# Scales of a tile moved ahead of its row transfers on GpSimd, and the weights of its sums applied by two small instructions, in a GroupNorm and patch top-k kernel

## The chip, the cores and the metric

One core of a Trainium2 chip. The metric is the device time of one launch in microseconds (us). Times of single instructions, and spans, come from one profiled execution.

## What is computed

x has shape (4, 256, 256, 256), float32: four images, 256 channels, 256 x 256 pixels.

```python
def _gn(v, G=32, eps=1e-5):
    g = v.reshape(B_, G, C_ // G, H_, W_)
    m, s = mean and variance of g over axes (2, 3, 4)
    return ((g - m) / sqrt(s + eps)).reshape(v.shape)

def _L0_conv_ref(x):               # P = 32, k = C // 2 = 128
    s = 0.5 * _grad_mag(x) + 0.5 * abs(x)
    sp = s.reshape(n, C, 8, 32, 8, 32).mean(axis=(3, 5)).reshape(n, C, 64)
    ranks = argsort(argsort(-sp, axis=1), axis=1)
    mask = ranks < k
    return x * mask, each mask value over its 32 x 32 patch

out = x + _L0_conv_ref(_gn(x))
```

`_grad_mag` is |x(h, w+1) - x(h, w-1)| + |x(h+1, w) - x(h-1, w)| with zeros outside the image. So for each of 64 patches of an image the 128 channels with the largest score get their normalized values added, and the others stay x.

## The kernel before

**Tiles.** A tile is 16 channels of one image, 8 bands of 32 rows each, so 128 partitions (channel and band) with 8 patches of 1024 pixels in a partition: 4096 KB. There are 16 tiles to an image and 64 in all. Four tile buffers (`ring`) are in turn loaded, worked on and stored by the sync queue. During the first eleven tiles it also sends copies of the last image's first tiles from input to output.

**The work of a tile.** VectorE takes the statistics (`bn_stats`), the inner horizontal differences (`inner_across`, L669), and reductions of what others prepare. TensorE forms vertical differences of five patches, ScalarE sums absolute values, GpSimd forms the vertical differences of the other three patches (`difference`, L320), the columns next to patch borders (`end_columns`, L328) and the edges. The 8 kinds of sums of a tile lie in `sums[tile % RING]`. `total` (L699, L703) multiplies them by a table of weights (1, except 2 for LARGER and -512 for MEANS) and adds them over the kinds. `score` multiplies by the tile's scale and puts out a score for each patch and channel.

**The scale.** VectorE's `minus_mean` (L660) opens a tile. GpSimd's `partition_spread` (L372, L374, L376, with a `drain` after the first two) makes the term of the variance, TensorE's `variance` averages it over the group, VectorE's `stable_variance` (L694) adds eps, and GpSimd's `scales` (L383 to L394, with five drains) raises to the power -1/2, refines that by one Newton step and stores the scale and the factors. TensorE's `variance` stands ahead of all its vertical differences of the tile, and `stable_variance` ahead of most of VectorE's work of the tile. VectorE waits for `scale_ready` of the tile before it overwrites `var` or makes the tile's score.

**The choice.** From the ninth tile of an image on, the 16 largest scores left of each patch are taken after each tile (`pick`, `choices`). The rows chosen go into `rows`, four columns of 128 row numbers to a block, 16 blocks to an image, 64 in all. For a block GpSimd gathers four times 128 rows of 4 KB from the input by indirect DMA (`gather_block`, L350), ScalarE scales them (`finish_place`, L570), and GpSimd scatters them to the output (`scatter_block`, L365). One block is gathered in each tile from the eleventh on, and one is scattered from the thirteenth on; the last ten blocks follow behind the last tile. The last four tiles of an image are dense: the kernel keeps them in the ring, ScalarE scales those that the choice names (`finish_dense`, L580) and they are stored in halves; rows of them are left out of the gathers. ScalarE's order of a tile begins with `o0`, the finish of the block that was gathered in the tile before, and its order holds three `p` steps, which need GpSimd's differences, and six `v` steps, which need TensorE's.

**Order on the queues.** Each engine works in the order written. On GpSimd it is the loop at L396. The sync queue, in each tile: store of this tile, perhaps a copy, the halves of the dense tile before, and the load of the tile three ahead; this load waits until the tile before is summed by ScalarE, is stored, and its differences and edges are read. Gathers and scatters go through the software queue, loads and stores through the hardware queue.

Of the kernel before, what the change touches and what calls it, by code (L numbers as in the profile page):

```python
# [8 lines left out]
ALU = mybir.AluOpType  # L9
# [10 lines left out]
PARTS = 128  # L20
# [52 lines left out]
ROWS = IMAGES * TILES * PARTS * COLS  # L73
LARGER, ENDS, MEANS, ACROSS_LAST, DOWN, CENTRED, ROWS_AT_EDGE, COLUMNS_AT_EDGE = range(8)
KINDS = 8
WEIGHTS = {LARGER: 2.0, MEANS: -2.0 * (BN // 2)}

ORDER = "o0 a0 o1 v0 o2 a1 o3 p0 a2 v1 a3 a4 v2 a5 p1 a6 v3 a7 v4 p2 v5".split()
ORDER_DENSE = ("o0 a0 o1 v0 o2 a1 o3 p0 a2 v1 a3 d0 d1 v2 d2 d3 a4 p1 d4 a5 v3 d5 d6 a6 d7 v4 a7 p2 v5"
# [36 lines left out]
def groupnorm_patch_topk(nc: bass.Bass, x: bass.AP, out: bass.AP):  # L116

    ctx = ExitStack()
    with ctx:
        def sb(name, shape, dt=FP32):  # L120
            return ctx.enter_context(nc.sbuf_tensor(name, shape, dt))
# [24 lines left out]
        same_band = sb("same_band", [PARTS, BANDS])  # L146
        same_band16 = sb("same_band16", [PARTS, BANDS], BF16)
        minus_half = sb("minus_half", [PARTS, 1])
        weights = sb("weights", [PARTS, KINDS])
        place_numbers = sb("place_numbers", [PATCHES, 1], INT32)  # L150
        first_row = sb("first_row", [PATCHES, 1])
        group_numbers = sb("group_numbers", [PARTS, 2, TILES], INT32)
# [2 lines left out]
        record = [sb(f"record{b}", [PARTS, 3]) for b in range(RING)]  # L155
        all_sums = sb("sums", [PARTS, RING, KINDS, COLS])
        sums = [all_sums[:, b] for b in range(RING)]
        weighed = sb("weighed", [PARTS, KINDS, COLS])
        totals = sb("totals", [PARTS, COLS])
        spread = sb("spread", [PARTS, 1])  # L160
        away = sb("away", [PARTS, 1])
# [69 lines left out]

        block = ctx.enter_context(nc.Block())

        CONSTANTS = 26 + len(WEIGHTS)

        x_rows = x.rearrange("t p (w f) -> (t p w) f", w=COLS)
        out_rows = out.rearrange("t p (w f) -> (t p w) f", w=COLS)
# [29 lines left out]
        def _(pool):  # L267
            steps = [0]

            def make(ins):  # L270
                steps[0] += 1
                ins.then_inc(constants, 1)
                pool.wait_ge(constants, steps[0])
# [8 lines left out]
            make(nc.gpsimd.memset(minus_half[:], -0.5))  # L282
            make(nc.gpsimd.memset(all_sums[:], 0.0))
            make(nc.gpsimd.memset(factors[:], 0.0))
            make(nc.gpsimd.memset(weights[:], 1.0))
            for kind, weight in WEIGHTS.items():
                make(nc.gpsimd.memset(weights[:, kind:kind + 1], weight))
            make(nc.gpsimd.memset(same_channel[:], 1.0))
            make(nc.gpsimd.memset(averager[:], 0.0))
            make(nc.gpsimd.memset(plus[:], 0.0))  # L290
# [23 lines left out]
            def difference(tile, k):  # L314

                m = POOL_DOWN * tile + k
                if m >= PLACES:
                    pool.wait_ge(place_free, m - PLACES + 1)
                v = patch(ring[tile % RING], PE_DOWN + k)
                nc.gpsimd.tensor_tensor(place[m % PLACES][:], v[:, 2 * PATCH:], v[:, 0:INSIDE], ALU.subtract)\  # L320
                    .then_inc(place_ready, 1)
# [47 lines left out]
            def partition_spread(tile):  # L369
                part_mean, part_var, nm = (record[tile % RING][:, k:k + 1] for k in range(3))  # L370
                pool.wait_ge(minus_mean_ready, tile + 1)
                nc.gpsimd.tensor_tensor(away[:], part_mean, nm, ALU.add)  # L372
                pool.drain()
                nc.gpsimd.tensor_tensor(newton[:], away[:], away[:], ALU.mult)  # L374
                pool.drain()
                nc.gpsimd.tensor_tensor(spread[:], newton[:], part_var, ALU.add).then_inc(spread_ready, 1)  # L376

            def scales(tile):
                nm = record[tile % RING][:, 2:3]
                now = scale[:, tile % RING:tile % RING + 1]  # L380
                made = factors[:, tile // TILES % 2, :, tile % TILES:tile % TILES + 1]
                pool.wait_ge(stable_var_ready, tile + 1)
                nc.gpsimd.tensor_tensor(rstd[:], var[:], minus_half[:], ALU.pow)  # L383
                pool.drain()  # L384
                nc.gpsimd.tensor_tensor(newton[:], rstd[:], rstd[:], ALU.mult)  # L385
                pool.drain()
                nc.gpsimd.tensor_tensor(correction[:], newton[:], var[:], ALU.mult)
                pool.drain()
                nc.gpsimd.tensor_scalar(newton[:], correction[:], -0.5, 1.5, ALU.mult, ALU.add)
                pool.drain()  # L390
                nc.gpsimd.tensor_tensor(now, rstd[:], newton[:], ALU.mult)
                pool.drain()
                nc.gpsimd.tensor_scalar(made[:, 0], now, 1.0, 1.0, ALU.mult, ALU.add)
                nc.gpsimd.tensor_tensor(made[:, 1], now, nm, ALU.mult).then_inc(scale_ready, 1)  # L394

            for tile in range(ALL_TILES):  # L396
                n = tile - LAG
                wait_loaded(pool, tile)
                partition_spread(tile)
                difference(tile, 0)  # L400
                if n >= 2:
                    scatter_block(n - 2)
                if n >= 0:
                    gather_block(n)
                scales(tile)
                end_columns(tile)
                difference(tile, 1)
                columns_at_edge(tile)
                difference(tile, 2)
                if tile == 1:  # L410
                    for s in range(SETS):
                        nc.gpsimd.memset(slots[s][:], 0.0).then_inc(slots_cleared, 1)
                    pool.wait_ge(slots_cleared, SETS)
# [221 lines left out]
        def _(dve):  # L635
# [54 lines left out]
            def stable_variance(tile):  # L690
# [2 lines left out]
                    dve.wait_ge(scale_ready, tile)  # L693
                nc.vector.tensor_scalar(var[:], var_bank, EPS, None, ALU.add).then_inc(stable_var_ready, 1)  # L694

            def total(tile):

                wait_summed(dve, tile)
                nc.vector.tensor_tensor(weighed[:], sums[tile % RING],  # L699
                                        weights[:].unsqueeze(2).broadcast_to([PARTS, KINDS, COLS]), ALU.mult)\  # L700
                    .then_inc(recorded, 1)
                settle()
                nc.vector.tensor_reduce(totals[:], weighed[:].rearrange("p k w -> p w k"), AX.X, ALU.add)  # L703

            def score(tile):
                r = tile % RING
# [80 lines left out]
            def step(tile):  # L787


                now, prev = tile < ALL_TILES, tile - 1  # L790
                ranked = prev >= 0 and prev % TILES >= FIRST_STEP
                if now:
                    inner_across(tile, (0, 1))
                else:
                    settle()
                if prev >= 0:
                    total(prev)
                if now:
                    stable_variance(tile)
                if prev >= 0:  # L800
                    score(prev)
                statistics(tile + 1, 0)
                if prev >= 0:
                    keep_scores(prev)
                if ranked:
                    pick(prev)
                statistics(tile + 1, 1)
                if ranked:
                    choices(prev)
                if now:  # L810
                    inner_across(tile, (2, 3, 4))
                    statistics(tile + 1, 2)
                    end_columns(tile)
                    statistics(tile + 1, 3)
                    inner_across(tile, (5, 6))
                    rows_at_edge(tile)
                    minus_mean(tile + 1)
                    columns_at_edge(tile)

            for part in range(3):  # L820
                statistics(0, part)
            dve.wait_ge(constants, CONSTANTS)
            statistics(0, 3)
            minus_mean(0)
            nc.vector.tensor_reduce(same_band[:], plus[:].rearrange("p (c b) -> p b c", b=BANDS), AX.X, ALU.add)
            nc.vector.tensor_copy(first_row[:], place_numbers[:])
# [24 lines left out]
```

## Time and profile before

| | |
|---|---|
| median of 2 runs | 2891.82 us (2890.99 to 2892.66) |
| the profiled execution | 2896.18 us, span 2894.4 us |
| TensorE matmul, busy | 1700.1 us (59%) |
| VectorE, busy | 1717.7 us (59%) |
| ScalarE, busy | 1601.7 us (55%) |
| GpSimd, busy | 1450.1 us (50%) |
| moved by DMA | 746.74 MB, mean 258 GB/s |

Busy time is the sum of an engine's instructions, without its waits, branches and semaphore work; a mean over the span hides that stages differ. DMA moves 396 to 407 GB/s in the first four of 40 slices of the span, and between 169 and 328 GB/s in most of the later ones. In the rows below, an idle time before an instruction is given with what ended it; `issue` says that the profile shows no releaser. POOL is GpSimd, DVE is VectorE, ACT is ScalarE, PE is TensorE, SPq is the sync queue.

### The profile page before, as it was taken

The page shows a single profiled execution, that of the slowest core. Times are in us where ns is not written, and L with a number is a line of the kernel's source. Part 1 is how long each engine was busy: PE and PEld are TensorE (multiplying, and loading weights), DVE is VectorE, ACT ScalarE, POOL GpSimd, SP SyncE. Part 2 cuts the span into 40 slices and gives each one's busy share as a digit, 9 for nine tenths or more (in the row PEclk, how much of TensorE's full clock was granted, in tenths as well). Part 3 has the DMA queues.
Part 4 walks back from the last instruction along what each step waited for, and adds up shares of the span by engine and source line. Part 5 has one row for each costly group of instructions (what it writes and reads, how often), then busy time and mean ns, then how long its engine had stood idle before and what let it go on. Part 6 is the DMA issues. An engine that isn't in the chain of part 4 may idle for free.

```text
span 2894.4 us, 18679 instructions
## 1 busy us (share of the span) xinstructions
PE 1700.1 (59%) x4304; PEld 829.2 (29%) x4304; DVE 1717.7 (59%) x3318; ACT 1601.7 (55%) x2561; POOL 1450.1 (50%) x1635
## 2 busy tenths in 40 slices
PE   6998576534655556755355555676647746567800
PEld 3444232212222223322122222333323322233300
DVE  8999586435554557755345464676636655568710
ACT  5776367534544446756345454556746645446953
POOL 7565265234454535634245353555435544446666
PEclk9999788766877788877687777788878868788955
DMA  9999856774746474566774646546765546465685
GB/s 396 397 407 405 368 198 265 307 312 192 289 181 273 176 278 189 215 255 265 308 297 193 262 193 249 213 174 253 282 269 210 218 181 273 169 253 193 243 326 192
DMA packets 95872, 746.74 MB, mean 258 GB/s; under 512 B 25256, under 2 KB 25256, under 8 KB 76176
## 3 DMA queue, kind: packets, MB, share of 16 engines
q1 hardware_dynamic: 22032, 536.88, 46.4%
q0 software_dynamic: 73728, 208.66, 18.6%
q8 instruction: 34, 0.56, 0.1%
q14 instruction: 78, 0.64, 0.1%
HBM read 427.82 MB, written 402.65 MB: 287 GB/s over the span
## 4 chain that ended last, share of the span: by engine, by line
issue 47%; POOL 20%; DVE 19%; POOLq 6%; DMA 4%; PE 2%; DVEq 1%; ACT 1%; another core or an unknown queue 0%; SPq 0%; ACTq 0%
DVE larger L669 9%; POOL slots L350 9%; POOL out_dram L365 6%; DVE stats L649 5%; POOLq L384 2%; POOL ends L328 2%; DMA ring<-in_x_dram 2%; DVEq L637 1%; DVE sums L676 1%; DVE sums L686 1%; DVE record L652 1%; POOL rstd L383 1%; DMA slots<-in_x_dram,rows 1%; POOL place L320 1%; PE vertical L512 1%
## 5 line engine op out<-in xcount | busy, mean ns | idle before, releaser
L512 PE MATMUL vertical<-ring,plus 128*128 128x512 f32 (+2 forms) x1536 | 860.8, 645 | 0.0
L513 PE MATMUL vertical<-ring,minus 128*128 128x512 f32 (+2 forms) x1536 | 813.8, 614 | 0.0
L599 ACT ACTIVATE place<-place 128x960 f32<-128x960 f32 x192 | 190.6, 993 | 1032.0 <-POOL place L320 1032.0
L669 DVE SCALAR_TENSOR_TENSOR larger<-ring 128x960 bf16<-128x960 f32 x448 | 627.1, 1441 | 16.3 <-issue 0.5
L649 DVE BATCH_NORM_STATS2 stats<-ring 128x6 f32<-128x512 f32 x1024 | 630.0, 677 | 10.1 <-DMA ring<-in_x_dram 9.9
L615 ACT ACTIVATE thrown<-ring,record 128x1024 bf16<-128x1024 f32 x512 | 581.6, 1136 | 1.6
L676 DVE TENSOR_REDUCE sums<-ends 128x7 f32<-128x448 f32 x64 | 39.5, 616 | 909.1 <-POOL ends L328 909.1
L475 PE MATMUL rank_bank<-record,averager 128*128 128x1 f32 x128 | 33.9, 334 | 886.4 <-DVE record L652 886.4
L385 POOL TENSOR_TENSOR newton<-rstd 128x1 f32<-128x1 f32 x64 | 12.3, 193 | 963.9 <-issue 962.5
L320 POOL TENSOR_TENSOR place<-ring 128x960 f32<-128x960 f32 x192 | 486.6, 2534 | 0.7 <-ACT place L599 0.7
L609 ACT ACTIVATE vertical<-vertical 128x960 f32<-128x960 f32 x384 | 365.1, 951 | 165.7 <-PE vertical L513 165.4
L513 PEld LDWEIGHTS vertical<-ring,minus 128*128 128x128 f32 x1536 | 322.6, 210 | 382.4 <-issue 382.4
L512 PEld LDWEIGHTS vertical<-ring,plus 128*128 128x128 f32 x1536 | 308.4, 214 | 259.1 <-issue 253.7
L570 ACT ACTIVATE slots<-slots,offset,factor 128x1024 f32<-128x1024 f32 x256 | 311.3, 1228 | 58.6 <-DMA slots<-in_x_dram,rows 58.6
L350 POOL DMA_INDIRECT slots<-in_x_dram,rows x256 | 283.2, 1106 | 80.4 <-issue 76.6
L365 POOL DMA_INDIRECT out_dram<-slots,rows x256 | 255.5, 998 | 89.3 <-issue 69.8
L475 PEld LDWEIGHTS rank_bank<-record,averager 128*128 128x128 f32 x128 | 29.4, 282 | 929.7 <-DVE record L652 911.9
L580 ACT ACTIVATE ring<-ring,coef 128x1024 f32<-128x1024 f32 x128 | 152.1, 1226 | 4.7 <-DVE coef L765 4.7
L699 DVE TENSOR_TENSOR weighed<-sums,weights 128x64 f32<-128x64 f32 x64 | 109.8, 1715 | 57.4 <-ACT vertical L609 57.4
L372 POOL TENSOR_TENSOR away<-record 128x1 f32<-128x1 f32 x64 | 12.3, 193 | 234.6 <-DVE record L660 234.5
L615 ACT ACTIVATION_READ_ACCUMULATOR thrown<-ring,record 128x1 f32 x512 | 96.2, 188 | 0.0
L338 POOL TENSOR_TENSOR edges<-ring 128x448 f32<-128x448 f32 x64 | 94.0, 1469 | 0.0
(97 smaller groups left out, 1334.7 us busy)
## 6 DMA issues: line engine op xcount, KB each, us to landing
ring<-in_x_dram SPq DMA_DIRECT2D x63, 4096.0 KB, 15.7
out_dram<-ring SPq DMA_DIRECT2D x42, 4096.0 KB, 26.1
out_dram<-ring SPq DMA_DIRECT2D x32, 2048.0 KB, 6.6
out_dram<-in_x_dram SPq DMA_DIRECT2D x12, 2048.0 KB, 56.4
ring<-in_x_dram SPq DMA_DIRECT2D x4, 1024.0 KB, 7.7
slots<-in_x_dram,rows POOLq DMA_INDIRECT x256, 17.0
out_dram<-slots,rows POOLq DMA_INDIRECT x256, 12.0
```

The costliest lines, as they stand in the source:

```text
L320: nc.gpsimd.tensor_tensor(place[m % PLACES][:], v[:, 2 * PATCH:], v[:, 0:INSIDE], ALU.subtract)\
L350: nc.gpsimd.indirect_dma_start(slot(n, j), None, x_rows, bass.IndirectOffsetOnAxis(ap=row, axis=0), bounds_check=ROWS - 1, oob_is_err=Fals ...
L365: nc.gpsimd.indirect_dma_start(out_rows, bass.IndirectOffsetOnAxis(ap=row, axis=0), slot(n, j), None, bounds_check=ROWS - 1, oob_is_err=Fa ...
L512: nc.tensor.matmul(to, plus[:], a, start=True, stop=False)
L513: done = nc.tensor.matmul(to, minus[:], b, start=False, stop=True)
L570: done = nc.scalar.activation(slot(n, j), slot(n, j), ACT.Identity, scale=factor[:, q:q + 1], bias=offset[:, q:q + 1])
L580: done = nc.scalar.activation(v, v, ACT.Identity, scale=made[:, 0, w:w + 1], bias=made[:, 1, w:w + 1])
L599: nc.scalar.activation(v, v, ACT.Abs, accum_out=sums[r][:, DOWN, w:w + 1])\
L609: nc.scalar.activation(v, v, ACT.Abs, accum_out=to).then_inc(vertical_free, 1)
L615: nc.scalar.activation(thrown[:], patch(buffer, k), ACT.Abs, bias=record[r][:, 2:3], accum_out=sums[r][:, CENTRED, k:k + 1]).then_inc(cent ...
L649: nc.vector.bn_stats(stats[:, k, :], buffer[:, k * BN:(k + 1) * BN])
L669: nc.vector.scalar_tensor_tensor(out=larger[w % 3][:].rearrange("p (r c) -> p r c", r=PATCH), in0=xs[:, w, :, 2:], scalar=0.0, in1=xs[:, w ...
```

## The change

In GpSimd's loop `scales(tile)` moves from behind the scatters and gathers to the place behind `partition_spread(tile)`, ahead of `difference(tile, 0)`. Its instructions and drains stay as they are. On VectorE the multiplication of all sums by the table of weights is left out, and with it the table, its buffer and three constants. In its place a new `weigh` multiplies seven columns of one kind in place: MEANS of the next tile ahead of `minus_mean`, and LARGER of this tile behind `columns_at_edge`, after a drain. `total` then reduces the sums themselves.

```diff
--- before.py
+++ after.py
@@ -73,7 +73,6 @@
 ROWS = IMAGES * TILES * PARTS * COLS
 LARGER, ENDS, MEANS, ACROSS_LAST, DOWN, CENTRED, ROWS_AT_EDGE, COLUMNS_AT_EDGE = range(8)
 KINDS = 8
-WEIGHTS = {LARGER: 2.0, MEANS: -2.0 * (BN // 2)}
 
 ORDER = "o0 a0 o1 v0 o2 a1 o3 p0 a2 v1 a3 a4 v2 a5 p1 a6 v3 a7 v4 p2 v5".split()
 ORDER_DENSE = ("o0 a0 o1 v0 o2 a1 o3 p0 a2 v1 a3 d0 d1 v2 d2 d3 a4 p1 d4 a5 v3 d5 d6 a6 d7 v4 a7 p2 v5"
@@ -146,7 +145,6 @@
         same_band = sb("same_band", [PARTS, BANDS])
         same_band16 = sb("same_band16", [PARTS, BANDS], BF16)
         minus_half = sb("minus_half", [PARTS, 1])
-        weights = sb("weights", [PARTS, KINDS])
         place_numbers = sb("place_numbers", [PATCHES, 1], INT32)
         first_row = sb("first_row", [PATCHES, 1])
         group_numbers = sb("group_numbers", [PARTS, 2, TILES], INT32)
@@ -155,7 +153,6 @@
         record = [sb(f"record{b}", [PARTS, 3]) for b in range(RING)]
         all_sums = sb("sums", [PARTS, RING, KINDS, COLS])
         sums = [all_sums[:, b] for b in range(RING)]
-        weighed = sb("weighed", [PARTS, KINDS, COLS])
         totals = sb("totals", [PARTS, COLS])
         spread = sb("spread", [PARTS, 1])
         away = sb("away", [PARTS, 1])
@@ -231,7 +228,7 @@
 
         block = ctx.enter_context(nc.Block())
 
-        CONSTANTS = 26 + len(WEIGHTS)
+        CONSTANTS = 25
 
         x_rows = x.rearrange("t p (w f) -> (t p w) f", w=COLS)
         out_rows = out.rearrange("t p (w f) -> (t p w) f", w=COLS)
@@ -282,9 +279,6 @@
             make(nc.gpsimd.memset(minus_half[:], -0.5))
             make(nc.gpsimd.memset(all_sums[:], 0.0))
             make(nc.gpsimd.memset(factors[:], 0.0))
-            make(nc.gpsimd.memset(weights[:], 1.0))
-            for kind, weight in WEIGHTS.items():
-                make(nc.gpsimd.memset(weights[:, kind:kind + 1], weight))
             make(nc.gpsimd.memset(same_channel[:], 1.0))
             make(nc.gpsimd.memset(averager[:], 0.0))
             make(nc.gpsimd.memset(plus[:], 0.0))
@@ -397,12 +391,12 @@
                 n = tile - LAG
                 wait_loaded(pool, tile)
                 partition_spread(tile)
+                scales(tile)
                 difference(tile, 0)
                 if n >= 2:
                     scatter_block(n - 2)
                 if n >= 0:
                     gather_block(n)
-                scales(tile)
                 end_columns(tile)
                 difference(tile, 1)
                 columns_at_edge(tile)
@@ -693,14 +687,16 @@
                     dve.wait_ge(scale_ready, tile)
                 nc.vector.tensor_scalar(var[:], var_bank, EPS, None, ALU.add).then_inc(stable_var_ready, 1)
 
+            def weigh(tile, kind, weight):
+
+                these = sums[tile % RING][:, kind, 0:ACROSS]
+                nc.vector.tensor_scalar(these, these, weight, None, ALU.mult)
+
             def total(tile):
 
                 wait_summed(dve, tile)
-                nc.vector.tensor_tensor(weighed[:], sums[tile % RING],
-                                        weights[:].unsqueeze(2).broadcast_to([PARTS, KINDS, COLS]), ALU.mult)\
+                nc.vector.tensor_reduce(totals[:], sums[tile % RING].rearrange("p k w -> p w k"), AX.X, ALU.add)\
                     .then_inc(recorded, 1)
-                settle()
-                nc.vector.tensor_reduce(totals[:], weighed[:].rearrange("p k w -> p w k"), AX.X, ALU.add)
 
             def score(tile):
                 r = tile % RING
@@ -814,13 +810,19 @@
                     statistics(tile + 1, 3)
                     inner_across(tile, (5, 6))
                     rows_at_edge(tile)
+                    if tile + 1 < ALL_TILES:
+                        weigh(tile + 1, MEANS, -2.0 * (BN // 2))
                     minus_mean(tile + 1)
                     columns_at_edge(tile)
+                    settle()
+                    weigh(tile, LARGER, 2.0)
 
             for part in range(3):
                 statistics(0, part)
             dve.wait_ge(constants, CONSTANTS)
             statistics(0, 3)
+            settle()
+            weigh(0, MEANS, -2.0 * (BN // 2))
             minus_mean(0)
             nc.vector.tensor_reduce(same_band[:], plus[:].rearrange("p (c b) -> p b c", b=BANDS), AX.X, ALU.add)
             nc.vector.tensor_copy(first_row[:], place_numbers[:])
```

## Rows read from the trace of the kernel before

**Rows 1.** Software DMA queue on the page: packets, MB, share of 16 engines.

```profile
q0 software_dynamic: 73728, 208.66, 18.6%
```

**Rows 2.** Sums of waits: engine, line, releaser, us, times, longest.

```profile
POOL newton L385 <- issue: 962.5, 54, 45.6
```

**Rows 3.** Timeline, one tile on GpSimd: start, us, instruction, idle before.

```profile
1487.67 0.19 POOL L372 TENSOR_TENSOR away<-record 128x1 f32<-128x1 f32 x1 [2.92 <-DVE record L660]
...
1488.34 1.08 POOL L376 TENSOR_TENSOR spread<-newton,record 128x1 f32<-128x1 f32 x1
1489.38 3.15 POOL L320 TENSOR_TENSOR place<-ring 128x960 f32<-128x960 f32 x1
1492.71 1.09 POOL L365 DMA_INDIRECT out_dram<-slots,rows  x1 [0.18 <-issue]
...
1502.81 0.99 POOL L350 DMA_INDIRECT slots<-in_x_dram,rows  x1 [0.30 <-issue]
1503.82 0.59 POOL L383 TENSOR_TENSOR rstd<-var,minus_half 128x1 f32<-128x1 f32 x1
1523.26 0.19 POOL L385 TENSOR_TENSOR newton<-rstd 128x1 f32<-128x1 f32 x1 [18.85 <-issue]
...
1524.92 1.30 POOL L328 TENSOR_TENSOR ends<-ring 128x448 f32<-128x448 f32 x1
1526.19 2.21 POOL L320 TENSOR_TENSOR place<-ring 128x960 f32<-128x960 f32 x1
...
1535.20 0.19 POOL L372 TENSOR_TENSOR away<-record 128x1 f32<-128x1 f32 x1 [2.92 <-DVE record L660]
```

**Rows 4.** Timeline, the same tile on VectorE and the sync queue.

```profile
1489.64 0.34 SPq L430 DMA_DIRECT2D ring<-in_x_dram  x1
...
1490.38 2.23 DVE L699 TENSOR_TENSOR weighed<-sums,weights 128x64 f32<-128x64 f32 x1
...
1492.90 0.15 DVE L694 TENSOR_SCALAR var<-rank_bank 128x1 f32<-128x1 f32 x1
...
1526.26 0.62 DVE L676 TENSOR_REDUCE sums<-ends 128x7 f32<-128x448 f32 x1 [22.22 <-POOL ends L328]
```

**Rows 5.** DMA queues from 1503 to 1506 us: packets, MB, share.

```profile
q1 hardware_dynamic: 41, 1.21, 93.6%
q0 software_dynamic: 37, 0.15, 12.3%
```

**Rows 6.** DMA queues from 1515 to 1518 us.

```profile
q0 software_dynamic: 479, 1.16, 97.4%
q1 hardware_dynamic: 1, 0.00, 0.0%
```

**Rows 7.** DMA queues from 1521 to 1524 us.

```profile
q0 software_dynamic: 44, 0.12, 10.2%
```

**Rows 8.** Windows of whole tiles, L372 alone (x tiles); PE clock, DMA share, GB/s.

```profile
17.10:274.00 256.90, 1.93 (x10) 0.98 1.00 402
274.00:369.20 95.20, 0.39 (x2) 0.80 0.84 349
...
1101.30:1177.00 75.70, 0.39 (x2) 0.86 0.54 208
...
1210.00:1307.60 97.60, 0.39 (x2) 0.79 0.65 258
1307.60:1440.60 133.00, 0.39 (x2) 0.69 0.74 300
1440.60:1868.20 427.60, 1.73 (x9) 0.77 0.59 233
2075.80:2177.10 101.30, 0.39 (x2) 0.76 0.67 270
...
2289.30:2576.70 287.40, 1.16 (x6) 0.77 0.57 226
```

**Rows 9.** Window of a tile behind a dense one, all engines (PE, PEld, DVE, ACT, POOL).

```profile
1177.00:1210.00 33.00, 26.89 (x74) 12.93 (x72) 30.32 (x66) 26.52 (x38) 22.66 (x25) 0.95 0.51 191
```

## The prediction

> **What bounds the kernel now.** I read the page's DMA queues first, then the sums of waits, then one ordinary tile in time order on GpSimd, the same tile on VectorE and the sync queue, then the traffic of both DMA queues in 3 us windows of it, then the windows that hold whole tiles, counted by GpSimd's first instruction of a tile (L372).
>
> The sums of waits show 962.5 us in front of L385, in 54 tiles, with no releaser [rows 2]. L385 is the instruction behind the first `drain` of `scales`. The ordinary tile shows what that drain waits for. L383 runs at 1503.82, straight behind the last gather, so arithmetic passes; L385 comes at 1523.26, 18.85 us later [rows 3]. The software queue moved 479 packets from 1515 to 1518 and its last 44 from 1521 to 1524 [rows 6, 7], and no gather or store is open behind that. So a drain behind row transfers waits until they have landed, here 35.6 us after the tile's first instruction at 1487.67 (call that s). Everything later in the tile (ends, two differences, edges) stands behind it, VectorE waits 22.22 us at L676 [rows 4], and the next tile starts 12 us after the landing, at s+47.5.
>
> Why does landing take so long? The tile's load and store (4096 KB each) go out at 1489.64 on the hardware queue [rows 4]. While both queues are active they are served packet by packet: 41 against 37 in 3 us, but the first are 1.21 MB and the second 0.15 MB [rows 5]. The software queue gets 12 packets per us then, and up to 160 once it is alone. A transfer has 144 packets (73,728 over 512 instructions [rows 1]), a tile 1,152. So nearly all row traffic lands after the hardware queue has emptied, about s+26 (it has one packet after 1515 = s+27.3 [rows 6]), however early it was issued. The 47.5 us are 26 of load and store, 9.6 of row traffic, 12 in which the DMA engines have nothing to do.
>
> **The move of scales.** Its drains leave the place behind the transfers. The next drain behind them is the first one of the next tile's `partition_spread` (between L372 and L374). I call the rest of the wait there D. Behind it stand PE's `variance` and all of its `inner`, VectorE's `stable_variance` and all its work of the tile, and GpSimd's own. ScalarE stands too, at o0, which needs the same gathers. So a tile lasts F + D, where F is the length without any drain wait.
>
> F, from rows: the variance was at s+5.2 with the 2.23 us multiply L699 ahead of it [rows 4]. Without it, with two further one-input instructions of 0.15 us (the cost of L694) and their settling, it comes at s+3.3. Scales take 2.4 (L383 0.59, drain, then 1.66 from L385 to L328), to s+5.8. Difference 0 took 3.15 beside the two-input multiply; 2.2 without (2.21 at 1526.19), to s+8.2. The eight transfers take 11.1 (1492.71 to 1503.80), to s+19.3. Before, ends began at s+18.4 without the wait (37.25 less 18.85), so this is 0.9 later. From L328 to the next s are 10.3 [rows 3]. F = 29.7, I take 30. The bounds are 29 and 31.5: the latter if difference 0 stays at 3.15 and the multiply's place on the way to var isn't won. In a tile behind a dense one, VectorE is busy 30.32 of 33.0 us [rows 9], so F is about 33 there, and nothing is gained.
>
> D, from rows: issue is 3.2 us later than now (difference 0 ends at s+8.2, not s+5), which leaves 3.2 x 12 = 38 more packets; together with the last 44 that landed after s+33.3 about 80 are open when the next load's data start. That load goes out at s'+2.0 (1489.64 for s' = 1487.67) and flows a good us later, here at s+33.5. The 80 packets now share the engines again. At 12 per us they need 7 us from s'+3.5, so D is about 10, and 8 if the issue costs less; if they sit on a few of the 16 engines they last until load and store are through, s'+26, D about 24. I take 16, the middle, since I have no row that shows the split by engine.
>
> A tile with D = 16 issues its own transfers at s+24 to s+35, when the hardware queue is already empty (s+26); 1,152 packets at 160 per us are through by s+38, ahead of its end at s+46. So the next tile has D = 0. **Tiles alternate**: 30 and 46, 38 on average, against 47.8.
>
> **The sum**, from the windows of whole tiles [rows 8]:
> - Ordinary tiles: nine in the window of 427.6 us, nine in the image before it, six in 287.4: 24 tiles of 47.8. 24 x 9.8 = 235 us.
> - Ten tiles with less traffic: the two in 75.7 us stand for all; one more such pair in each later image, one tile in the first, three in the last. Now 37.8; 31.5 without spill, some start spilled; 4 each: 40 us.
> - The pairs at an image's end, 97.6 us, three times: same landing, 10.8 per tile, 65 us.
> - The image starts, 133.0 (twice) and 101.3: queues hold more work there, and only the dead time between landing and the next load is won, from 1523.3 to 1537.2 (2.0 behind L372 at 1535.20) = 14 us a tile. Six tiles, 84 us.
> - The two tiles in 95.2 us: the first lands no earlier (its queue is behind from the copies), the second wins one dead time: 15 us.
> - The ten tiles without gathers (256.9 us) have no drain wait, and their DMA is at 402 GB/s with a share of 1.00. VectorE would be some 2 us a tile quicker without L699, but loads then become late: 2 us in all.
> - Tiles at 33.0: nothing. The tail after the last tile's start has no scales and stays.
>
> Together 441 us. From the profiled execution's 2896.2 us that leaves 2455; the median of the runs is 4.4 lower, so 2450.
>
> **The weights.** L699 goes, with its 2.23 us; that it and GpSimd's difference 0 (3.15 against 2.21) hold each other up is a reading of these two rows, and both are in F. L703's reduction reads the sums directly, at the same shape. In tiles with gathers neither instruction is on the path by itself: the DMA cycle covers them. The two new instructions cost 0.15 each from L694; the one ahead of `minus_mean` is on the path (in F), the other, after `columns_at_edge`, ahead of var. Should they wait for GpSimd, the nearest price is L376's 1.08 us [rows 3], an instruction of one column beside VectorE's two-input work; from 0 to 1.1 per tile, and I take 0, because GpSimd idles 2.92 us ahead of L372, where the first of them falls [rows 3]. The Trainium skill, SBUF — State Buffer, section Who interferes with whom, says that `tensor_scalar` may enter a mode that takes the pair of ports shared with GpSimd, so that it blocks or is blocked, while an instruction with one input outside that mode is free. By it up to 1.1 us for each of 64 tiles, 70 us, would be added, and only where DMA doesn't cover it; no row shows it, since L694 (0.15 us) reads PSUM. Leaving out three constants ahead of the first tile is nothing: the first load covers it.
>
> **Rivals.**
> *No spill.* The last packets are through before the next load flows. For it: just 44 packets were left at s+33.3. Against: later issue. Ordinary tiles then last 32: 15.8 x 24 = 379, the ten 60, the pairs 89, the rest as above 99: 627, so 2265. Chance 0.12.
> *Full spill, every second tile.* The rest always waits until the next load and store are through: D = 26, average 43; 115 + 0 + 30 + 60 + 15 = 220, so 2670. Chance 0.12.
> *The wait stays.* It isn't the drain that is held but any but the first instruction behind transfers; the trace shows only L383 pass, in every tile. Then ends waits for landing. 1.66 us of scales come off behind it, and 3.2 us of later issue come on, if landing follows issue. 54 tiles: from -89 to +84. Since the row traffic waits for the hardware queue, nearer the first: 2820. Chance 0.07.
> *Slower: spill in every tile.* If a tile with a large D doesn't catch up, because its transfers too land only behind the next load and store, each tile lasts 30 + 24 = 54. It decides from D = 18 in every tile (30 + 18 is the present length). 24 x 6.2 = 149 more and 30 in the pairs: 3070. Against it: from s+26 on, the hardware queue is empty, and 20 us are left. Chance 0.06.
>
> **How the numbers follow.** The forecast has 0.63. With D = 8 an average tile has 34: 96 more, 24 in the pairs, 15 in the ten: 2315. With D = 24 it has 42: the same less, 2590. The range 2310 to 2670 takes in both, and the full spill at its edge; no spill, the slower case and the stay are outside it, in part or whole. Faster by over 2% (below 2834, about what a measurement tells from no change): 0.63 + 0.12 + 0.12 and 0.02 of the stay, 0.89. Within 2%: 0.04. Slower: 0.06 and 0.01, 0.07.
>
> **What would show it.** The 962.5 us ahead of L385 gone, some 250 to 300 us ahead of L374 in its place; ScalarE at L570 and PE behind the variance waiting with it; ordinary tiles alternating, about 30 and 46, not equal ones; L320 at 2.2 us throughout (it has 3.15 for difference 0 now); DMA share from 0.59 to over 0.7 in those windows; the last packets of a tile moved beside the next tile's load. All equal at 32, or at 54, would make me wrong on D; a wait ahead of L328, on what the drain does.

## The result, and the profile after

The changed kernel takes 2331.6 us (median of 2 runs, 2330.4 to 2332.9) against 2891.8: a ratio of 0.806, 95% interval 0.804 to 0.808. Its profiled execution has a span of 2328.7 us.

The sums of waits of the changed kernel (engine, what waited, releaser, us, times, longest):

```profile
PE rank_bank L474 <- POOL spread L370: 381.6, 58, 38.7
...
POOL newton L368 <- issue: 264.9, 53, 36.2
...
ACT slots L564 <- issue: 211.7, 27, 35.6
DVE var L688 <- PE rank_bank L474: 190.7, 38, 34.4
```

The 962.5 us behind the power instruction [rows 2] are gone. What is left of the wait stands ahead of L368, the instruction behind the first drain of `partition_spread`: 264.9 us. TensorE's variance, VectorE's `var` and ScalarE's finish of the gathered rows wait for the same moment.

An ordinary tile on GpSimd, in time order, to be laid beside [rows 3]:

```profile
772.97 0.19 POOL L366 TENSOR_TENSOR away<-record 128x1 f32<-128x1 f32 x1 [2.99 <-DVE record L654]
774.81 0.19 POOL L368 TENSOR_TENSOR newton<-away 128x1 f32<-128x1 f32 x1 [1.65 <-issue]
...
777.04 0.58 POOL L377 TENSOR_TENSOR rstd<-var,minus_half 128x1 f32<-128x1 f32 x1 [0.98 <-DVE var L688]
...
779.42 2.21 POOL L314 TENSOR_TENSOR place<-ring 128x960 f32<-128x960 f32 x1
781.81 1.09 POOL L359 DMA_INDIRECT out_dram<-slots,rows  x1 [0.19 <-issue]
...
792.55 0.99 POOL L344 DMA_INDIRECT slots<-in_x_dram,rows  x1 [0.30 <-issue]
793.56 1.36 POOL L322 TENSOR_TENSOR ends<-ring 128x448 f32<-128x448 f32 x1
...
803.98 0.19 POOL L366 TENSOR_TENSOR away<-record 128x1 f32<-128x1 f32 x1 [2.99 <-DVE record L654]
```

The drain ahead of L368 waits 1.65 us. The scale's chain starts at s+4.1 (777.04 less 772.97), difference 0 takes 2.21 us and starts at s+6.4, the transfers are issued from s+8.8 to s+20.6, ends follow at once, and the next tile starts after 31.0 us instead of 47.5. The load of this tile, on the sync queue, and then the two DMA queues, first in the 4 us of this tile from 797 on, then in the first 3 us of the next tile, 804 to 807 (packets, MB, share):

```profile
773.54 0.34 SPq L424 DMA_DIRECT2D ring<-in_x_dram  x1
```

```profile
q0 software_dynamic: 462, 1.11, 69.9%
```

```profile
q1 hardware_dynamic: 16, 0.52, 60.6%
q0 software_dynamic: 61, 0.20, 16.8%
```

The load goes out at s+0.6, not s+2.0 [rows 4]. At s+24 the hardware queue is through and the software queue has the engines alone, as in [rows 6]. 61 of its packets pass in the next tile's first 3 us: 52 of them before 805.4, where the next load's first packets come, and 9 beside it.

Whole tiles, counted by GpSimd's first instruction (GpSimd busy, TensorE clock as a share of full speed, DMA share, GB/s); the windows answer to those of [rows 8], with that of 33.0 us in [rows 9] as the fourth:

```profile
17.20:275.70 258.50, 1.93 (x10) 0.98 1.00 403
275.70:364.20 88.50, 0.39 (x2) 0.77 0.87 363
897.30:973.00 75.70, 0.39 (x2) 0.86 0.57 220
973.00:1011.90 38.90, 0.19 (x1) 0.80 0.52 203
1011.90:1076.80 64.90, 0.39 (x2) 0.93 0.88 350
1076.80:1162.90 86.10, 0.39 (x2) 0.80 0.98 408
1162.90:1478.90 316.00, 1.74 (x9) 0.84 0.83 328
1659.60:1726.70 67.10, 0.39 (x2) 0.95 0.93 376
1834.90:2020.10 185.20, 1.16 (x6) 0.89 0.88 349
```

Tiles are counted from 0. The nine ordinary tiles of 427.6 us (tiles 34 to 42) take 316.0, of which tile 34 alone takes 64.5; the six of 287.4 take 185.2, the pair of 97.6 takes 64.9, the image start of 133.0 takes 86.1. Two of these windows didn't gain: the pair of 75.7 us (tiles 27 and 28) takes 75.7, and the tile of 33.0 (tile 29) takes 38.9.

### The profile page after: what moved, and what is told of

The parts are those of the page before. It is cut to its first block, busy times and chain, and to the rows that moved or that the text cites. A ratio compares the mean times of both kernels' runs of the same rounds, so it can differ in the third digit from the quotient of the medians.

```text
span 2328.7 us, 18741 instructions
## 1 busy us (share of the span) xinstructions
PE 1660.0 (71%) x4304; PEld 814.2 (35%) x4304; DVE 1677.7 (72%) x3382; ACT 1603.5 (69%) x2561; POOL 1416.5 (61%) x1632
## 4 chain that ended last, share of the span: by engine, by line
DVE 39%; issue 24%; POOL 16%; PE 7%; POOLq 5%; DMA 4%; DVEq 2%; ACT 1%; SPq 0%; ACTq 0%
DVE larger L663 17%; DVE stats L643 12%; POOL slots L344 7%; POOL out_dram L359 5%; PE vertical L506 3%; PE vertical L507 3%; DMA ring<-in_x_dram 3%; DVEq L631 2%; POOL ends L322 2%; POOLq L367 2%; DVE record L646 1%; DVE sums L680 1%; POOLq L369 1%; DVE sums L670 1%; DMA slots<-in_x_dram,rows 1%
## 5 line engine op out<-in xcount | busy, mean ns | idle before, releaser
L506 PE MATMUL vertical<-ring,plus 128*128 128x512 f32 (+2 forms) x1536 | 842.0, 632 | 0.0
L507 PE MATMUL vertical<-ring,minus 128*128 128x512 f32 (+2 forms) x1536 | 799.5, 604 | 0.0
L663 DVE SCALAR_TENSOR_TENSOR larger<-ring 128x960 bf16<-128x960 f32 x448 | 664.4, 1524 | 16.0 <-issue 1.3
L314 POOL TENSOR_TENSOR place<-ring 128x960 f32<-128x960 f32 x192 | 440.4, 2294 | 0.0
L344 POOL DMA_INDIRECT slots<-in_x_dram,rows x256 | 297.8, 1163 | 77.9 <-issue 77.6
L359 POOL DMA_INDIRECT out_dram<-slots,rows x256 | 271.3, 1060 | 91.2 <-issue 70.3
L474 PE MATMUL rank_bank<-spread,averager 128*128 128x1 f32 x128 | 30.9, 311 | 381.6 <-POOL spread L370 381.6
L593 ACT ACTIVATE place<-place 128x960 f32<-128x960 f32 x192 | 190.8, 994 | 129.5 <-POOL place L314 129.5
L368 POOL TENSOR_TENSOR newton<-away 128x1 f32<-128x1 f32 x64 | 35.1, 548 | 266.5 <-issue 264.9
L474 PEld LDWEIGHTS rank_bank<-spread,averager 128*128 128x128 f32 x128 | 28.2, 271 | 427.8 <-issue 427.6
L688 DVE TENSOR_SCALAR var<-rank_bank 128x1 f32<-128x1 f32 x64 | 9.9, 154 | 190.7 <-PE rank_bank L474 190.7
L670 DVE TENSOR_REDUCE sums<-ends 128x7 f32<-128x448 f32 x64 | 38.9, 608 | 97.8 <-POOL ends L322 97.6
```

The costliest lines, as they stand in the source:

```text
L344: nc.gpsimd.indirect_dma_start(slot(n, j), None, x_rows, bass.IndirectOffsetOnAxis(ap=row, axis=0), bounds_check=ROWS - 1, oob_is_err=Fals ...
L359: nc.gpsimd.indirect_dma_start(out_rows, bass.IndirectOffsetOnAxis(ap=row, axis=0), slot(n, j), None, bounds_check=ROWS - 1, oob_is_err=Fa ...
L506: nc.tensor.matmul(to, plus[:], a, start=True, stop=False)
L507: done = nc.tensor.matmul(to, minus[:], b, start=False, stop=True)
L593: nc.scalar.activation(v, v, ACT.Abs, accum_out=sums[r][:, DOWN, w:w + 1])\
L663: nc.vector.scalar_tensor_tensor(out=larger[w % 3][:].rearrange("p (r c) -> p r c", r=PATCH), in0=xs[:, w, :, 2:], scalar=0.0, in1=xs[:, w ...
```

## The experiments

Below, "before" and "after" are the two kernels. Every ratio is to before, with its 95% interval. A short diff leaves out what is the same.

**1. The move alone.** Before, with only this:

```diff
                 partition_spread(tile)
+                scales(tile)
                 difference(tile, 0)
...
                     gather_block(n)
-                scales(tile)
```

> Only scales is moved; the multiply of all sums by the weights stays as before. Theory A (the move takes the drains away from the row transfers, and that is the gain): 2350 to 2430 us. The variance comes some 2 us later in each of the 54 tiles with gathers, so up to 100 us of the 560 are given back, less where DMA or another engine sets the tile's length. The 962 us wait behind the power instruction is gone, some 250 us stand in partition_spread instead. Theory C (the multiply by weights, which contends with GpSimd, was what mattered): above 2750.

2318.1 us, ratio 0.802 (0.799 to 0.805), 32 us below the range for theory A. So the move is the whole gain, as far as these intervals tell, and the up to 100 us expected back for the old weights didn't come. The reason is in the multiply (min, median and max of its duration in ns, then its first and last start in us):

```profile
L699 DVE TENSOR_TENSOR weighed<-sums,weights x64: 217/222/227, 45.0 to 2168.7; 128x64 f32<-128x64 f32 x64
```

Its 2.23 us in [rows 4] end 0.1 us after GpSimd's difference 0, beside which it runs, so most of it had been a wait for that. Once scales stand there, no long GpSimd instruction runs beside it, and it takes 0.22.

**2. The weights alone.** After, with `scales` back behind the transfers (the diff of experiment 1, reversed).

> Only the weights are changed; scales stays behind the transfers. Theory A: the tile is still 26 us of load and store, 9.6 of rows and 12 behind the landing, all set by load and store, not by VectorE: 2860 to 2895 us, the wait behind the power instruction near 960 us or a little more, since the transfers are issued up to 1 us earlier. Theory C: below 2750.

2889.5 us, ratio 0.999 (0.998 to 1.000), and the wait as it was:

```profile
POOL newton L379 <- issue: 956.7, 54, 45.0
```

Theory C falls with experiments 1 and 2 together: the move alone brings the gain, and the weights alone bring none.

**3. One drain more.** After, with a drain that orders nothing:

```diff
                 if n >= 0:
                     gather_block(n)
+                    pool.drain()
```

> The changed kernel with one drain more, straight behind the gathers of a tile and ahead of the ends, with nothing to order there. Theory A (a drain behind row transfers is held until they have landed): the wait is back in its old place, some 17 us in each of 54 tiles, and with it nearly the old time, 2850 to 2920 us; transfers are issued 3 us later than before, the scale's chain of 1.7 us is off. Theory B (a drain costs what it does elsewhere, 0.15 us, and something else about the position of scales counted): 2331 to 2345 us.

2856.3 us, ratio 0.987 (0.985 to 0.989), inside the range for theory A: one instruction gives 525 of the 560 us back. Its wait, at the first instruction behind it:

```profile
POOL ends L322 <- issue: 804.1, 54, 40.7
```

54 waits, 14.9 us on average. That is shorter than the 17.8 of before because the drain stands about 3 us later in the tile now, and the landing didn't move with the issue. Over 22 ordinary tiles (the 24 without tiles 18 and 34) the first transfer was issued at s+8.1 to s+8.4 instead of s+5.0, and the last packet of the rows was through 34.5 us after s, against 34.9 in before (medians; the hardware queue's large packets ended at s+25.4 and s+26.4). So 3 us of later issue cost half a microsecond of landing at most.

**4. No move, no drains in scales.** Before, with each drain of `scales` replaced by a semaphore:

```diff
+            def follow(ins):
+                ins.then_inc(pooled, 1)
+                done_here[0] += 1
+                pool.wait_ge(pooled, done_here[0])
...
-                nc.gpsimd.tensor_tensor(rstd[:], var[:], minus_half[:], ALU.pow)
-                pool.drain()
+                follow(nc.gpsimd.tensor_tensor(rstd[:], var[:], minus_half[:], ALU.pow))
```

> The kernel before with scales in its old place, but each of its five drains replaced by a semaphore that the instruction ahead of it raises and GpSimd waits for. Theory A: arithmetic behind transfers is not held, only drains are; the 962 us wait goes without any move, and the tile is set by F of about 30 us and the next tile's drain in partition_spread: 2330 to 2450 us. Theory B' (whatever follows the first instruction behind transfers is held until they land): 2850 to 2900 us, with the wait at the same instruction.

2321.9 us (runs from 2294 to 2336), ratio 0.797 (0.792 to 0.802), with nothing moved; the median is 8 us below the range for theory A. Arithmetic behind the transfers runs and can even be waited for; the drain is what is held. In the sums of waits the power instruction's successor no longer appears, and what is left is the next tile's first drain:

```profile
POOL newton L381 <- issue: 296.9, 53, 37.4
```

Theory B' falls, and experiment 3 had ruled out theory B. Together they show the cause from both sides.

**5. Semaphores in place of all seven drains of a tile**, in after (`follow` as above, in `partition_spread` too).

> The changed kernel with all seven drains of a tile on GpSimd (two in partition_spread, five in scales) replaced by semaphores. Theory A: no wait for landing is left on GpSimd, so PE no longer stands behind the variance. What is left is ScalarE at its first step, which needs the gathered rows, and loads that come late. The 265 us of drain wait are mostly hidden then, but ScalarE's stand holds PE after three vertical results, so only part comes back: 2240 to 2310 us. Rival D (ScalarE's wait for the same rows is worth as much as the drain's): 2310 to 2335 us.

2272.5 us, ratio 0.784 (0.780 to 0.788), inside the range for theory A. GpSimd has no such wait any more; the rows' landing now shows at ScalarE, and through it at TensorE:

```profile
ACT slots L564 <- issue: 374.3, 24, 34.9
...
PE vertical L506 <- ACT vertical L603: 236.6, 46, 29.1
```

**6. The finish later as well.** Experiment 5, with ScalarE's order changed (and the dense order in the same way):

```diff
-ORDER = "o0 a0 o1 v0 o2 a1 o3 p0 a2 v1 a3 a4 v2 a5 p1 a6 v3 a7 v4 p2 v5".split()
+ORDER = "a0 a1 v0 a2 v1 a3 p0 a4 v2 o0 a5 o1 o2 o3 p1 a6 v3 a7 v4 p2 v5".split()
```

> As the kernel with semaphores throughout, and ScalarE's four finishing steps of a gathered block stand after its first seven to nine other steps of a tile, so nothing at the start of a tile needs the rows. Theory A: another 30 to 100 us less, in the tiles where rows land 15 to 40 us into the next tile: 2150 to 2280 us. If DMA sets those tiles (the queues are full for the whole of them), the time moves by less than 20 us against the one with semaphores alone.

2200.2 us, ratio 0.763 (0.760 to 0.766). Another 72 us, within 30 to 100. What still waits for the rows are the tiles in which they land very late:

```profile
ACT slots L564 <- DMA slots<-in_x_dram,rows: 228.8, 24, 40.9
```

**7. Transfers ahead of difference 0**, in after:

```diff
                 scales(tile)
-                difference(tile, 0)
                 if n >= 2:
                     scatter_block(n - 2)
                 if n >= 0:
                     gather_block(n)
+                difference(tile, 0)
```

> The changed kernel with the scatters and gathers of a tile ahead of its first difference, so issued 2.2 us earlier. If rows land only when the hardware queue has emptied, the landing doesn't move: 2315 to 2345 us, drain wait 230 to 290 us. If landing follows issue (what the rivals with a later issue assumed): the drain wait of ordinary tiles, 2 to 3 us, goes, 24 tiles by 2 us: 2270 to 2300 us.

2471.5 us, ratio 0.855 (0.854 to 0.856): neither expectation, although the drain wait, 258.8 us, lies in the first one's range. The edit did a second thing. Difference 0 now stands behind the transfers, some 13 us later, and ScalarE's step `p0` waits for it (129.5 us of such waits in after):

```profile
ACT place L593 <- POOL place L314: 434.8, 62, 10.1
```

and so ScalarE sums up each tile later, and the load, which waits for that, goes out at s+4.7 instead of s+0.6:

```profile
736.15 0.19 POOL L366 TENSOR_TENSOR away<-record 128x1 f32<-128x1 f32 x1 [2.99 <-DVE record L654]
...
740.88 0.34 SPq L424 DMA_DIRECT2D ring<-in_x_dram  x1
```

In the dense tiles, where ScalarE has most to do, tiles last 40 us instead of 33. In ordinary ones the transfers were issued from s+8.0 at the earliest instead of about s+8.8, but in most the drain behind the rows let go 37 to 39 us after s instead of 33 to 34. The run doesn't hold everything else still, but in it landing moved with the load, and against the issue.

**8. Small stores.** After, where the whole-tile stores write an eighth of each tile, so the output is incomplete:

```diff
-                sp.dma_start(out[tile], ring[tile % RING][:]).then_inc(stored[tile % RING], 16)
+                sp.dma_start(out[tile, :, 0:AREA], ring[tile % RING][:, 0:AREA]).then_inc(stored[tile % RING], 16)
```

> The changed kernel with the whole-tile stores of the sync queue cut to an eighth (one patch column of 1024 of the 8192), so that about half of the hardware queue's traffic is gone in ordinary tiles; the output outside that part isn't written. Theory A: in ordinary tiles the length stays at F, 30 to 31 us, since only 2 to 3 us of landing stuck out; the tiles at 45 to 64 us (the eight with a drain wait of 16 to 36 us) fall to about 31, 150 to 190 us in all, and the first eleven tiles lose some us: 2100 to 2190 us. Rival E (the long tiles are long for another reason than the queue's backlog): 2300 us or more.

2198.4 us, ratio 0.760 (0.759 to 0.762), 8 us over the range for theory A. Tiles 11, 17 and 18 of this kernel:

```profile
308.80:342.60 33.80, 0.19 (x1) 0.90 0.46 187
519.00:550.30 31.30, 0.19 (x1) 0.90 0.89 358
550.30:597.30 47.00, 0.19 (x1) 0.75 0.60 236
```

They had lasted 55.4, 52.2 and 56.1 us in after. Of the eight long tiles five fall to 30 to 34; tiles 18 and 34 keep 47 and 46, and tile 50 its 47. They stand one or two tiles behind those in which the dense tiles' halves are stored, which this edit leaves as they are. Ordinary tiles stay at 30.3 to 31.2. So the five are the queues' backlog. For the three that keep their length this run doesn't show it; that the stores of halves hold them is not tried. In the ordinary ones landing had cost about 0.5 us a tile (30.7 us on average against 31.2).

**9. Gaps between GpSimd's instructions behind the transfers**, in after:

```diff
                 end_columns(tile)
+                pool.wait_ge(ends_ready, tile + 1)
                 difference(tile, 1)
+                pool.wait_ge(place_ready, POOL_DOWN * tile + 2)
                 columns_at_edge(tile)
+                pool.wait_ge(edges_ready, tile + 1)
                 difference(tile, 2)
```

> The changed kernel with GpSimd's four instructions behind the transfers (ends, difference, edges, difference) parted: each waits for the semaphore that the one ahead of it raises. Theory F (GpSimd's unbroken row of instructions holds a two-input instruction of VectorE for its whole length, 7 to 9 us in seven tiles, 48 us in all; before the change the drain wait kept the two apart): a VectorE instruction that has to wait waits for one of GpSimd's only, at most 3.3 us; the tiles at 39 us fall to about 34: 2290 to 2320 us. Rival G (the long instruction is held by the row transfers or by something that these gaps don't touch): 2325 to 2345 us, and instructions of over 4 us remain.

2306.6 us, ratio 0.797 (0.795 to 0.800), 25 us less than after and inside theory F's range; none of VectorE's 448 inner instructions takes over 3.5 us, where after had seven over 4. All of its six runs, 2293 to 2324 us, are below after's two, but two are few, so the size is less certain than the sign. The gaps did a second thing that the expectation hasn't got. In many tiles GpSimd's last difference now runs beside the new `weigh` that stands ahead of `minus_mean`, and 35 of the 128 instructions of `weigh` take 1.3 us or more instead of 0.17 (one in after), 51 us more in all. This one is through when the difference beside it ends:

```profile
459.00 1.57 DVE L696 TENSOR_SCALAR sums<-sums 128x7 f32<-128x7 f32 x1
457.53 3.02 POOL L314 TENSOR_TENSOR place<-ring 128x960 f32<-128x960 f32 x1
```

So what parting the row is worth by itself stays open; the gaps with the old multiply of the weights were not tried. The row that they part is shown in the next section.

**10. The gaps in the kernel of experiment 6.**

> The kernel with semaphores throughout and the later finish, with the same gaps. It has three instructions of VectorE over 4 us, 17 us in all, so theory F gives 10 to 20 us: 2180 to 2195 us; rival G: 2200 us as before.

2192.8 us, ratio 0.7574 (0.7565 to 0.7584), 7 us less than experiment 6 and inside theory F's range. Its longest inner instruction takes 3.2 us, but 47 of the 128 instructions of `weigh` are held as in experiment 9, 68 us in all. This is the fastest version: 24.3% below before, 6% below after.

**11. The load later**, in after:

```diff
                 if RING <= tile + RING - 1 < ALL_TILES:
+                    sp.wait_ge(recorded, tile)
                     load_tile(tile + RING - 1)
```

> The changed kernel with each load of the sync queue, and the store behind it, held back until VectorE has formed the sums of the tile before, about 3.2 us into a tile instead of 0.5. The prediction put D, the landing beyond the start of the next tile, at 16 us in every second tile for a load at 2.0 us. If D is that sensitive to when the load goes out: ordinary tiles alternate, 36 to 38 us on average, 2440 to 2500 us. If landing only shifts with the load: 2 to 3 us more in 24 tiles and about as much in the long ones, 2390 to 2430 us.

2320.2 us, ratio 0.802 (0.798 to 0.805): neither expectation, and no slower than after. The load goes out at s+3.2. The drain's successor in two tiles that follow each other, s being 746.41 and 781.89:

```profile
753.29 0.19 POOL L368 TENSOR_TENSOR newton<-away 128x1 f32<-128x1 f32 x1 [6.68 <-issue]
...
784.17 0.81 POOL L368 TENSOR_TENSOR newton<-away 128x1 f32<-128x1 f32 x1 [2.08 <-issue]
```

Ordinary tiles do alternate now, 35.5 and 31.1 us here, but with D = 6 and 2, 33 us on average, not 38. The landing did shift with the load: 35.4 us after s against 32.9 in after (medians of the 22 ordinary tiles). Those tiles last 29 us longer in all, and elsewhere as much came back: tile 27, at 44.7 us in after, takes 30.5.

## Why the prediction was right, and where it was off

**Mechanism.** "A drain behind row transfers waits until they have landed" is shown by experiments 3 and 4. That the wait would reappear in `partition_spread`, with TensorE, VectorE and ScalarE behind it, is what the waits of after show. That their sum, 264.9 us, lies in the 250 to 300 forecast is luck: it was to come from spills in every second ordinary tile, and 184 us of it stand in eight tiles with 16 to 36 us each (11, 17, 18, 27, 33, 34, 43, 50).

**F.** 30 us was forecast; after has 31.0 in the tile above with 1.65 us of drain wait in it, so F is about 29.4. Its parts came near: var at s+3.3 (3.8), transfers to s+19.3 (20.6), L320 at 2.2 us in place of 3.15.

**D, the term that was mis-sized.** "I take 16, the middle, since I have no row that shows the split by engine" and with it "Tiles alternate: 30 and 46". Measured, L368 comes 1.6 to 3.7 us into most ordinary tiles, so D is 1.3 to 3.4, and 21 of the 22 last 30 to 32 us one like another. By the prediction's own sign ("all equal at 32") it was wrong on D there. Three things were wrong in it. The later issue was to leave "3.2 x 12 = 38 more packets", but in experiment 3 rows issued 3 us later landed no later in the tile. The load goes out at s+0.6 and not at s'+2.0, so the hardware queue is through sooner, at s+23 instead of s+26. And so nearly all packets left over pass before the next load's data come, as the windows above show (52 and 9); even with a load at s+3.2 (experiment 11) D doesn't pass 7 in the 22 ordinary tiles. The rival "no spill" described the ordinary tiles, with 32 us; it missed the image starts and three lighter tiles.

The sharing that the prediction feared does occur, in these other tiles. When the load of tile 27 brings its first packets, at s+1.5, some 140 packets of rows are still to come. From s+4 to s+15 of it (901.4 to 912.4) the queues moved:

```profile
q1 hardware_dynamic: 123, 3.54, 74.6%
q0 software_dynamic: 17, 0.05, 1.1%
```

and the drain lets go at s+16.4, when the hardware queue is through as well. Tiles 27, 43 and 50 have waits of 16.2, 16.4 and 18.1 us, about the D that was taken for every second ordinary tile.

By class, before less after, forecast in brackets: the 24 ordinary tiles 1146.3 - 806.3 = 340 us (235), of which two, tiles 18 and 34, last 56 and 64 in after; the three pairs at an image's end 97 (65); the three image starts 121 (84); the ten lighter tiles 18 (40); the pair with the copies' backlog 7 (15); the first ten tiles -2 (2); the five at 33 us -16 (0). Together 565, against 441. So the time fell into the range with some luck too: the ordinary tiles, the pairs and the image starts gained 174 us more than forecast, and the others 50 us less.

**The image starts** follow the reading given: queues hold more there, and the wait is pushed on from tile to tile (D of 24 and 28 us in tiles 17 and 18, 24 and 36 in tiles 33 and 34), with the DMA share at 0.98. Experiment 8 shows that tiles 17 and 33 are the queues' backlog; tiles 18 and 34 kept 47 and 46 us there.

**Two classes that I had wrong.** The lighter tiles were put at 31.5, with 4 us taken off for some spilled starts, and of the tiles of 33 us it said "nothing". The first class gained 18 us and not 40 because tiles 27, 43 and 50, with the waits just shown, last 45 to 47 us, and tile 60 lasts 38.8. In tile 60, and in tiles 13, 29 and 45 of 33 us, which last 39, time is lost by an effect that the prediction hasn't got. VectorE's inner instruction with two inputs in tile 29 (start, us):

```profile
992.84 7.79 DVE L663 SCALAR_TENSOR_TENSOR larger<-ring 128x960 bf16<-128x960 f32 x1
```

and GpSimd beside it:

```profile
992.20 1.35 POOL L322 TENSOR_TENSOR ends<-ring 128x448 f32<-128x448 f32 x1
993.50 2.21 POOL L314 TENSOR_TENSOR place<-ring 128x960 f32<-128x960 f32 x1
995.67 1.35 POOL L332 TENSOR_TENSOR edges<-ring 128x448 f32<-128x448 f32 x1
...
997.39 2.21 POOL L314 TENSOR_TENSOR place<-ring 128x960 f32<-128x960 f32 x1
```

An instruction of 1.16 us (at 1194.71 in the trace of before it was that) takes 7.79: it starts 0.6 us after ends, stands through the five GpSimd instructions behind ends, and is through 1.0 us after the last of them, at 1000.63. Seven such instructions took 48 us more than 1.16 each in after, six took 41 more in experiment 1. Before has none: in the tiles with gathers its GpSimd stood in the drain while VectorE got to this point. Experiment 9 shows it by parting the row. The Trainium skill, SBUF — State Buffer, section Who interferes with whom, says that a VectorE instruction with two SBUF inputs contends with a GpSimd one that reads SBUF, and that the pair of ports which they share is an exclusive lock. The trace agrees on the pair of instructions, and shows the hold going on through the whole row.

The rule named in the prediction, on `tensor_scalar`, cost next to nothing in after, where 127 of the 128 new instructions took 0.15 to 0.17 us. But it shows. The one that fell beside GpSimd's clearing of the slots took 4.05 us and was through when that ended, at 70.66 (both in tile 1, which the DMA sets):

```profile
66.64 4.05 DVE L693 TENSOR_SCALAR sums<-sums 128x7 f32<-128x7 f32 x1
60.25 10.41 POOL L406 MEMSET slots<- 128x4096 f32 x3
```

With the gaps of experiments 9 and 10 it held 35 and 47 of them.

**The weights.** "Both are in F" gave the removal of the multiply some 2 us a tile of F. Experiment 1 has that without it: the move had already parted the multiply from difference 0. In the first ten tiles 2 us in all were forecast, since the DMA sets them: they take 258.5 us against 256.9, so nothing came there.

**Open.** Why the rest of the rows gets stuck in one tile and not in its like isn't settled. Tile 27 takes 44.7 us in after, 31.1 with the move alone, 30.5 in experiment 11; and the number of packets left doesn't decide it alone, since tile 43 of the move alone had 136 left beside its load and a wait of only 5.7 us. The runs of one kernel also spread over some 23 to 43 us in experiments 1, 4, 5, 9 and 11, which fits tiles that tip either way, but was not tried. After and the move alone (ratios 0.806 and 0.802) have intervals that overlap.

## What to carry to other kernels

Behind indirect transfers on GpSimd, don't order arithmetic by a drain: a semaphore that the instruction itself raises orders it without waiting for the rows. If the drains must stay, put them where the transfers have landed, and look which engines stand behind the first one that comes after. When a long wait is removed, look at what it had kept apart: here it let a row of GpSimd's instructions run into VectorE's two-input ones. Three gaps in the row gave some of it back, and moved GpSimd's last difference onto another VectorE instruction.

## What the runs showed of the hardware

- A drain on GpSimd behind indirect transfers is held until they have landed, 14.9 us on average in experiment 3, up to 45.6 us before; an arithmetic instruction, and a wait for its semaphore, is not (experiment 4).
- While both DMA queues had work, they moved nearly equal numbers of packets, 41 and 37 in 3 us, with 1.21 against 0.15 MB [rows 5]. So rows of 4 KB beside whole-tile transfers got a ninth of the traffic, and most landed when the others were through. Issued 3 us later they landed no later (34.5 us after s against 34.9, experiment 3); with the load 2.6 us later they landed 2.5 us later (35.4 against 32.9, experiment 11).
- A two-input VectorE instruction was held 7.79 us by a row of GpSimd instructions without a gap; with a semaphore wait between them no such instruction took over 3.5 us.
- A VectorE `tensor_scalar` of 128 x 7 elements in SBUF takes 0.17 us by itself and was held until GpSimd's instruction beside it ended: 4.05 us beside a memset, about 1.57 us beside a difference (experiment 9).
- The same multiply of 128 x 64 elements takes 0.22 us beside idle or short GpSimd work, and 2.23 us beside a long difference.
